# The message stage's source rows: one broadcast transfer from DRAM in place of two PE products per step

## The reference

```python
# layer 1: the list of edges is taken twice, forward and with both ends exchanged
src_full, dst_full = concat([src, dst]), concat([dst, src])
edge_in = concat([nf[src_full], nf[dst_full], ef_full], axis=-1)     # 128 + 128 + 64 columns
msg = leaky_relu(edge_in @ We1) @ We2                                # hidden width 256
red = segment_sum(msg, dst_full, num_segments=N)                     # sum at the receiving node
out = x + leaky_relu(concat([nf, red]) @ Wn1) @ Wn2
```

## Time and profile before

| | |
|---|---|
| median of three runs | 5955.15 us (5943.6 to 5958.23) |
| the profiled execution's own time | 5968.85 us |
| its span, first to last instruction | 5967.0 us |
| message stage in that span | 3127 to 5818 us |
| PE, DVE, ACT, POOL busy, share of the span | 61%, 65%, 24%, 63% |
| mean granted TensorE clock | 0.758 of full speed |
| moved by DMA | 836.72 MB, 140 GB/s over the span |

### The profile page before, as it was taken

How to read it: one execution, slowest core, us unless ns; L and a number is a source line. 1 busy time by engine, 2 the same in 40 slices (tenths; PEclk the granted TensorE clock), 3 DMA queues, 4 the chain that set the end, 5 groups by cost and what they waited for, 6 DMA issues and landing times. The chain is left out here.

```text
span 5967.0 us, 110677 instructions
## 1 busy us (share of the span) xinstructions
PE 3616.4 (61%) x18587; PEld 2574.6 (43%) x18588; DVE 3898.3 (65%) x11908; ACT 1442.3 (24%) x3070; POOL 3782.6 (63%) x3803
## 2 busy tenths in 40 slices
PE   0153333333314777771558788788778787888877
PEld 0122222222214666661425555555555455555546
DVE  4644444444427666668947777777777777777774
ACT  0120000000004555553332222222222222222222
POOL 3136655565555777765217788888887788878770
PEclk9875565555555555555679999998999999899899
DMA  2254444444423555543157788888887888888874
GB/s 54 62 159 116 111 113 109 114 116 114 108 66 98 130 129 130 130 119 110 47 161 172 173 178 183 178 182 175 180 178 174 179 180 179 179 178 179 178 153 136
DMA packets 895552, 836.72 MB, mean 140 GB/s; under 512 B 228060, under 2 KB 752636, under 8 KB 895257
## 3 DMA queue, kind: packets, MB, share of 16 engines
q0 software_dynamic: 217200, 396.10, 32.2%
q1 hardware_dynamic: 641257, 406.10, 25.1%
q10 hardware_dynamic: 37008, 33.70, 2.4%
HBM read 597.83 MB, written 237.64 MB: 140 GB/s over the span
## 5 line engine op out<-in xcount | busy, mean ns | idle before, releaser
L1543 POOL DMA_INDIRECT sums<-msg_bsum,k_sidx x831 | 1323.3, 1592 | 303.3 <-issue 261.4
L725 POOL DMA_INDIRECT max_xe<-rows,max_idx x832 | 786.1, 945 | 710.9 <-ACT max_idx L797 401.8
L1678 PEld LDWEIGHTS msg_both_ps<-msg_onehot,msg_hid 128*128 128x128 f32 x3712 | 562.4, 208 | 1222.4 <-issue 832.0
L1557 POOL DMA_INDIRECT msg_ga<-ab,k_bsrc x832 | 826.0, 993 | 369.9 <-issue 200.6
L1691 PE MATMUL msg_pre_ps<-msg_rw,msg_lt 128*128 128x512 f32 x1856 | 1047.7, 648 | 8.8 <-DMA msg_rw<-ab 8.8
L1643 ACT ACTIVATE msg_low_ps<-msg_xs 128x512 f32<-128x512 f32 x928 | 558.1, 601 | 2012.7 <-DVE msg_xs L1612 1033.3
L1678 PE MATMUL msg_both_ps<-msg_onehot,msg_hid 128*128 128x64 f32 x3712 | 616.0, 292 | 520.4 <-DVE msg_bsum L1587 338.8
L956 POOL TENSOR_SCALAR att_keyhot<-k_ramp,att_keys 128x128 f32<-128x128 f32 x1028 | 611.6, 611 | 276.2 <-ACT att_keys L1028 276.2
L1611 DVE TENSOR_TENSOR msg_xs<-msg_pre_ps,msg_ga 128x256 f32<-128x256 f32 x928 | 390.8, 421 | 532.1 <-PE msg_pre_ps L1691 219.5
L1622 DVE TENSOR_TENSOR msg_hid<-msg_xs,msg_low_ps 128x512 f32<-128x512 f32 x928 | 637.0, 686 | 106.4 <-issue 40.2
L1068 PE MATMUL att_sum_ps<-att_px,att_keyhot 128*128 128x136 f32 x2056 | 559.0, 453 | 220.5 <-DVE att_px L990 215.3
(11 more groups left out here) (296 smaller groups left out, 6031.3 us busy)
## 6 DMA issues: line engine op xcount, KB each, us to landing
msg_rw<-ab SPq DMA_DIRECT2D x928, 128.0 KB
l_outside<-xe SPq DMA_DIRECT2D x1028, 72.0 KB, 2.5
xe<-max_xe SPq DMA_DIRECT2D x104, 576.0 KB
att_keyrow<-key ACTq DMA_DIRECT2D x257, 128.0 KB, 3.3
msg_lt<-in_efT SPq DMA_DIRECT2D x928, 32.0 KB
rows<-node_rows SPq DMA_DIRECT2D x50, 288.0 KB, 2.4
max_begin<-begin SPq DMA_DIRECT2D x104, 128.0 KB
max_xe<-rows,max_idx POOLq DMA_INDIRECT x832
```

Source lines behind the costliest of these rows:

```text
L725: pool.indirect_dma_start(xe[:, b, u, :], None, T.rows, bass.IndirectOffsetOnAxis(ap=idx[:, b, u:u + 1], axis=0)).then_inc(s_xe[b], 16)
L1543: pool.indirect_dma_start(T.sums[k % 2], bass.IndirectOffsetOnAxis(ap=K.sidx[:, k:k + 1], axis=0), bsum[:, (k + 1) % SB, :], None, compute ...
L1557: pool.indirect_dma_start(ga[:, (k + 1) % RB, :], None, T.ab, bass.IndirectOffsetOnAxis(ap=K.bsrc[:, k:k + 1], axis=0)).then_inc(s_ga[k % ...
L1678: pe.matmul(fwd_ps[u % 2][:, q * WIN:(q + 1) * WIN], hid[:, b % 2, u, HID + q * P:HID + (q + 1) * P], onehot[:, b, u, :], start=True, stop ...
```

## The change

The sources of a block are read from `T.blk` with a step of zero over the partitions: one transfer per step takes one row of 512 B to all 128 partitions of `srow`. SP issues four per group, after the window rows of the same group, on the same semaphore (`s_rw`, now 32 per step and buffer use). The comparison reads `srow` in SBUF instead of `src_ps` in PSUM and waits for `s_rw`; so does PE's product, whose wait now covers both kinds of transfer. The two products per step, the copy into `hl`, the table `src_hl` and the four conversions that made it are gone. The diagonal of 128 is still used by `relation_maxima` (L835) and is made there.

```diff
@@ edge_inputs, DVE
-            L.mark(dve.tensor_scalar(part[:, :], K.src[:, 0:STEPS], 7, None, ALU.arith_shift_right))
-            L.mark(dve.tensor_copy(K.src_hl[:, :, 0], part[:, :]))
-            L.link(dve.tensor_scalar(part[:, :], K.src[:, 0:STEPS], P - 1, None, ALU.bitwise_and))
-            L.mark(dve.tensor_copy(K.src_hl[:, :, 1], part[:, :]))
+            L.wait()
@@ edge_messages
-        src_ps = ph.ps("src_ps", [P, U, P])
+        srow = ph.sb("srow", [P, 2, U, P])
...
+            def sources(j, b):
+                e = registers(nc, sp, mybir.EngineType.SP, K.reg_e, j * U, U, BLOCKS * P)
+                if past(j, 2):
+                    sp.wait_ge(s_same, j - 1)
+                    settle(sp, K)
+                for u in range(U):
+                    sp.dma_start(srow[:, b % 2, u, :], T.blk[ds(e[u] >> 7, 1), 0:P].to_broadcast([P, P])).then_inc(s_rw[b % 2], 16)
...
-            pipeline(sp, GROUPS, RG, [(0, features), (0, windows)])
+            pipeline(sp, GROUPS, RG, [(0, features), (0, windows), (0, sources)])
@@ hots, DVE
-                dve.tensor_copy(hl[:, b, :, :], K.src_hl[:, k, :])
@@ compare, DVE
-                dve.wait_ge(s_tr, j + 1)
+                dve.wait_ge(s_rw[b % 2], (j // 2 + 1) * 32 * U if isinstance(j, int) else (j - b % 2) * 16 * U + 32 * U)
...
-                dve.tensor_tensor(same[:, b % 2, :, :], src_ps[:, :, :],
+                dve.tensor_tensor(same[:, b % 2, :, :], srow[:, b % 2, :, :],
@@ transpose, PE
                 if past(j, 1):
                     pe.wait_ge(s_oT, j)
-                    pe.wait_ge(s_same, j)
...
-                for u in range(U):
-                    pe.matmul(src_ps[:, u, :], hl[:, b, u, 0:1].to_broadcast([P, P]), K.identb128[:, :], start=True, stop=False)
-                    last = pe.matmul(src_ps[:, u, :], hl[:, b, u, 1:2].to_broadcast([P, P]), K.identb[:, :], start=False, stop=True)
@@ steps, PE
-                pe.wait_ge(s_rw[b % 2], (j // 2 + 1) * 16 * U if isinstance(j, int) else (j - b % 2) * 8 * U + 16 * U)
+                pe.wait_ge(s_rw[b % 2], (j // 2 + 1) * 32 * U if isinstance(j, int) else (j - b % 2) * 16 * U + 32 * U)
```

More of the change, by code:

```diff
@@ L242, in _ @@
             L.mark(dve.tensor_scalar(K.identb[:, :], K.ramp[:, 0:P], K.part[:, 0:1], None, ALU.is_equal))
-            L.mark(dve.tensor_scalar(K.identb128[:, :], K.ramp[:, 0:P], K.part[:, 0:1], float(P), ALU.is_equal, ALU.mult))
             L.mark(dve.tensor_scalar(K.upto[:, :], K.ramp[:, 0:P], K.part[:, 0:1], None, ALU.is_le))
@@ L677, in relation_maxima @@
         real = ph.sb("real", [P, 1])
+        identb128 = ph.sb("identb128", [P, P], BF16)
         hl = ph.sb("hl", [P, 2, G, 2], BF16)
@@ L733, in _ @@
             part, end = K.sidx, slice(BLOCKS - 1, BLOCKS)
+            L.mark(dve.tensor_scalar(identb128[:, :], K.ramp[:, 0:P], K.part[:, 0:1], float(P), ALU.is_equal, ALU.mult))
             L.mark(dve.tensor_copy(srcf[:, :], K.bsrc[:, :]))
@@ L834, in sources @@
                         v = q * G // 2 + u
-                        pe.matmul(src_ps[q][:, u, :], hl[:, b % 2, v, 0:1].to_broadcast([P, P]), K.identb128[:, :],
+                        pe.matmul(src_ps[q][:, u, :], hl[:, b % 2, v, 0:1].to_broadcast([P, P]), identb128[:, :],
                                   start=True, stop=False)
@@ L1372, in edge_inputs @@
         inside = ph.sb("inside", [P, STEPS])
-        part = ph.sb("part", [P, STEPS], I32)
         row0 = ph.sb("row0", [P, P])
@@ L1475, in edge_messages @@
         SUM_LAG, ADD_LAG = 2, 3
-        hl = ph.sb("hl", [P, RG, U, 2], BF16)
         onehot = ph.sb("onehot", [P, RG, U, WIN])
@@ L1661, in transpose @@
                     pe.wait_ge(s_oT, j)
-                    pe.wait_ge(s_same, j)
                 settle(pe, K)
                 for u in range(U):
-                    pe.transpose(oT_ps[:, u * P:(u + 1) * P], onehot[:, b, u, :], K.ident[:, :])
-                for u in range(U):
-                    pe.matmul(src_ps[:, u, :], hl[:, b, u, 0:1].to_broadcast([P, P]), K.identb128[:, :], start=True, stop=False)
-                    last = pe.matmul(src_ps[:, u, :], hl[:, b, u, 1:2].to_broadcast([P, P]), K.identb[:, :], start=False, stop=True)
+                    last = pe.transpose(oT_ps[:, u * P:(u + 1) * P], onehot[:, b, u, :], K.ident[:, :])
                 last.then_inc(s_tr, 1)
@@ L1862, in build @@
         K.ident, K.upto, K.ones = ph.sb("ident", [P, P]), ph.sb("upto", [P, P]), ph.sb("ones", [P, P])
-        K.identb, K.identb128 = ph.sb("identb", [P, P], BF16), ph.sb("identb128", [P, P], BF16)
+        K.identb = ph.sb("identb", [P, P], BF16)
         K.headmask, K.trash = ph.sb("headmask", [P, H]), ph.sb("trash", [P, 1])
@@ L1888, in build @@
             K.reg_l = l1.sb("reg_l", [1, P * KB], I32)
-            K.src_hl = l1.sb("src_hl", [P, STEPS, 2], BF16)
             h1T = l1.sb("h1T", [P, NP])
```

## The result

The changed kernel takes 6072.97 us (median of four runs, 6060.28 to 6086.44), the kernel before beside it 5956.44: a ratio of 1.0211, 95% interval 1.0175 to 1.0247. It is 116.5 us slower; the prediction was 5949, with 6015 as its upper end. The profiled execution took 6072.43 us.

A forecast was written before the change was run, and what follows sets the result against it. POOL's own issuing of scatters and gathers was taken to set the message stage's length. Terms -12 + 2.5 + 3 = -6.5 us on the profiled execution, 5968.85 us, carried over to the runs' median: 5949 us; range for all 5922 to 6015.

The forecast's parts named there:

- Data: DMA in the message stage: 60.8 MB more at 33 ns per packet, share 0.81 to 0.90, nothing saturating on average.
- B: Rival, message stage: sources land late for the comparison or SP's issue takes too long; +70 us, 6025 us; chance 0.13.
- PE: Message stage: removed products free 0.5 to 1.1 us of a group's 11.6, under POOL's round, worth nothing by itself.
- DVE: Message stage: the copy goes, 0.18 us per group; the comparison stays at 681 ns; the gain lies under POOL's round.
- What that gives back: POOL's waits for DVE in the message stage: 16.5 us can be had, -12 us taken, ends 0 and -17.
- SP's queue: Four more issues per group cost 3.24 us and fit SP's 3.5 to 5.2 us of waiting for PE.
- Landing: Source transfers land in 3.3 us, 0.75 us ahead of the comparison in a tight group: 0 us; upper bound 4.6.
- Opening: Start of the message stage: first comparison and product need sources too, +2.5 us before the first scatter.
- POOL beside DVE: Message stage: a second two-SBUF comparison per group meets POOL's instructions; +3 us, between +9.7 and -6.
- rival C: Message stage: the SBUF comparison holds up POOL's instructions through the port, 38 us in place of +3; 5984 us; chance 0.13.
- A: Rival: all POOL's waits for DVE and the meetings go and the tail gains; -24 us, 5931 us; chance 0.17.
- D: Rival: PE, with less to do, is granted less clock; +30 us, 5985 us; chance 0.05.

The follow-up runs named there:

- unread transfers: The kernel before plus the 928 source transfers into a buffer nobody reads, though PE waits for them; 6028.7 us, 1.0145 on the first chip.
- half: The changed kernel with each source row sent to partitions 0 to 63 only, half the bytes; 6010.43 us, 0.9963 to the kernel before on the second chip.
- double: The changed kernel with source rows of 256 numbers instead of 128, twice the bytes; 6148.55 us, 1.0202 to the kernel before on the second chip.
- the order ahead of the windows: The changed kernel with SP issuing the source transfers before the window transfers; 6082.1 us, 1.0104 to the kernel before on the second chip.
- three tables: The changed kernel with three tables of sums, scatter k waiting for k-3 instead of k-2; 5940.89 us, 0.9985 (first chip); 5952.74, 0.9861 (third).

## Why the prediction was wrong

**The step that failed** stands under *Data*: "Nothing saturates on average; POOL hardly waits for a landing". Both halves were true of the kernel before. But the landing of scatter k-2 had a median of 2.2 us, one in ten above 3.2, against 3.5 of room, and I priced no growth of it: the sum had no term for what the new packets do to the scatters' landings. With the change 145 scatters have a wait for a sum or a landing in front of them, where 33 had one before. Price on the first chip: 86 us (unread transfers) or 95 (changed kernel less the one without transfers); again some 95 by half and double on the second, with the reservation above. No rival had it; B looked at the new transfer's own landing, not at what it does to the others.

**Point by point.**

*POOL as the bound*: right, and the reason for the whole loss. *PE* and *DVE*: right; the comparison takes 685 ns (681 before) and PE's removed products gave POOL nothing. On the first chip DVE got ahead by the full ring with the transfers alone and with the change without its transfers, so either is enough.

*What that gives back*, -12: right in kind. On the first chip it is at most the 17 allowed. On the others it is worth more, since POOL waits more for DVE there. Why the DVE-PE loop is slower on those chips stays open.

*SP's queue*: right. The wait for PE fell to 1.7 us per group (394.7 / 232), where 1 to 2 was predicted:

```profile
SPq L140 <- PE msg_pre_ps L1690: 394.7, 93, 7.9
```

*Landing* of the sources: DVE waited 32.6 us for them and PE 35.7, neither on the path, as the order ahead of the windows shows.

*Data*: queue 1 has 133632 packets more, the 118784 foreseen and 16 closing ones for each of 928 transfers. Queue 1 took (0.297 x 6070.6 - 0.251 x 5967.0) x 16 = 4880 us more of engine time, 305 per engine against the 245 of the text. The 33 ns per packet were right: from 3200 to 5700 us the 512-byte packets, features and sources together, took 33.0 ns on the mean. The rest is the closing packets and queue 1's other packets, which got longer (2 KB ones from 112.8 to 119.5 ns). The share is 0.86, not 0.90, because the stage got longer and POOL's packets took less time; with three tables it is the 0.90 predicted.

*Opening*, +2.5: from first gather to first scatter 36.7 us before and 37.5 after (3088.2 to 3125.7), so +0.8 in one profile each. That the stage starts 15 us earlier is not the change: the kernel before has its first scatter at 3140.4 in one profile and 3120.3 in another.

*POOL beside DVE*, +3: right in kind, too small. The lengths grew by 17 us with the changed kernel's waits and by 30 without them. Without the two-SBUF comparison the first chip's time is 43 us lower, known to 24 us; on the second, with the comparison on ACT, it is 7 lower, known to 24 as well. So rival C's mechanism is there; its price (38) fits the first chip's 43 and not the second's 7, where the comparison on ACT has costs of its own. How much of the time it is stays open. Whether it is more than the 17 us of lengths wasn't settled; a longer POOL instruction also delays the landing that the next but one waits for, which fits and was only argued. The Trainium skill ("SBUF — State Buffer", "Who interferes with whom") has the direction right: a DVE instruction with two SBUF inputs contends with a GpSimd instruction that reads SBUF.

*Rivals.* A and D fell (clock 0.91 against 0.92). B fell (30 waits of the comparison for its sources). C came in part: scatters' and gathers' means are 1604 and 1001 ns, where 1610 and 1000 were its sign. The sum with the experiments' sizes on the first chip: -12 + 1 + 43 + 86 = 118, against 116.5. That it fits so closely is luck: 43 and 86 are each known to some 20 us, and the -12 wasn't measured.

## What to carry to other kernels

A wait that never shows in the profile still has a margin; before adding traffic, find each transfer that the bounding engine waits for, and set its landing time against the time it has. If the margin is thin, deepen that buffer first: here a third table turned a loss of 0.4% into a gain of 1.4% on one chip, and one of 2.1% into a gain of 0.15% on another. When two engines each seem to wait for the other, look for the third thing that releases both. And where two limits are nearly equal, the worth of relieving one depends on the chip: measure on more than one.

## What the hardware showed

- More load didn't lengthen the packets of POOL's queue: they took 61.1% of 16 x 700 us for 48526 packets before, 141 ns each, and 56.6% for 46254 after, 137 ns; the scatters' own, of 1 KB, went from 132 to 125 ns. The scatters lose their time around their packets: by the count of packets a scatter's first one started 2.2 us after the issue began before and 2.4 after, and from its first to its last it took 1.5 us and 2.0 (medians).
- Moving the same transfers from SP's queue to ACT's made the latest landings later and the kernel 1.9% slower still (1.0233 against 1.0040). The Trainium skill ("DMA: Bandwidth & Descriptors", "Queues, rings and completion order") says that each engine takes turns between the queues that have work. A third queue would then give POOL's a smaller part of the turns. A tenth of the landings above 4.2 us, not 3.7, at a lower DMA share (0.82) agrees with that; a median of 2.6 us, not later than 2.8, doesn't. No run here shows the turns themselves.
- A comparison of 128 x 512 with both operands in SBUF took 685 ns, as with one in PSUM; POOL's instructions beside it got longer (1592 to 1604 and 993 to 1001 ns on the mean with the waits of the changed kernel; 1619 and, without the one gather of 14.07 us, 1002 in the version without transfers). In the changed kernel the 87 gathers that ran beside a comparison took 1067 ns on the mean, the others 993.
- Chips ran the same kernel 1.4% apart (5948 and 6029 us). Two profiles of the kernel before (spans 5967.0 and 5997.5 us) differ by 50 us between first and last scatter.
